# Attended values of two sets made back to back, and a turned-probability buffer of eight units instead of four

## The chip, the core and the metric

The kernel runs on one core of one Trainium2 chip. The metric is the device time in microseconds (us) of one execution. Five engines work side by side: TensorE (PE; its weight loads have a row of their own, PEld), VectorE (DVE), ScalarE (ACT), GpSimd (POOL) and SyncE (SP), which issues the transfers.

## The reference

Seven attention stages run one after the other on x, of shape (8 batches, 112 tokens, 256), with a context of shape (8, 375, 192). Stages 0, 2 and 5 attend to x itself, stages 1, 3, 4 and 6 attend to the context; a feed-forward part follows stages 1, 3 and 6.

```python
h = layer_norm(x)
q = (h @ Wq).reshape(B, 112, 16, D); k = (ctx @ Wk).reshape(B, 375, 16, D); v = (ctx @ Wv).reshape(B, 375, 16, D)
attn = softmax(einsum('bnhd,bshd->bhns', q, k) * scale)
out  = einsum('bhns,bshd->bnhd', attn, v)          # the attended values
x = out.reshape(B, 112, 16 * D) @ Wo + bo + x
```

Stages 1, 3 and 4 are the large cross stages: 16 heads of D = 64 with 375 keys. The change is about them.

## The kernel before

All work is cut into events, and every engine runs a list of them in a fixed order. The order of TensorE is written out by `tensor_order` (L414). The orders of the other engines come from `plan` (L563), which plays the events through with assumed durations. On each engine it takes the event that can start first, and among those that can start at once the one with the smallest value of ready time minus a head start (`AHEAD`, L496). The head start is 2.5 for the copies of turned probabilities (`trans`) and for the value and query evictions, and 0 for the exponentials (`scores`). So on a busy ScalarE these copies go ahead of exponentials.

A unit of a large cross stage is one head of one batch. A set is four units, so a batch has four sets. In this text slot s.b.i is the stretch of TensorE's list from set i of batch b in stage s up to the next set; i = 0 and 2 are the even slots, i = 1 and 3 the odd ones. A unit goes through this chain:

1. `set`: TensorE makes the scores of four units into the four PSUM banks pS, two pairs of units one after the other. From batch 2 on, each unit takes three matmuls (64 rows, 376 columns). A pair may start when ScalarE has read the four-units-older scores out of its banks (`bank_read`, L1192).
2. VectorE takes the maximum (L1826), ScalarE the exponential and its sum (L1696, into P), VectorE the reciprocal (L1850), GpSimd the scaling of P (L1969).
3. `trans`, in the slot after the set: TensorE turns P into a bank of pG in three transposes (L1512), and ScalarE copies it to the turned probabilities PT (L1709). The copy waits until the set that used the same part of PT has been attended (L1704).
4. `av`: TensorE multiplies the turned probabilities of a set with the values V into the bank pO (64 columns of the array for each head, two heads side by side, 24 matmul records in a set). Two sets fill the bank; then ScalarE and VectorE take it out (`ao`, L1715 and L1862).

Between these stands other work (`fill`): keys of the next batch (`k`, `kk`), queries, values (`v`, `vp`), the output projection of an older batch (`wo`). It shares the three banks of pG in turn with the transposes: an event may start when the event three places before it has been evicted (`work_start`, L1324). One piece of the values of each half (`m` = 1) is made in pO, between the two uses of that bank by `av`, at the end of the odd slots (`vp`).

The list `held` in `tensor_order` decides where `av` stands. In slot n stands the `av` of the set before the last one, directly behind the scores of slot n: every slot has one. Two neighbouring slots of TensorE's list, as before has them:

```
set3.4.0 av3.3.2 trans3.3.12 trans3.3.13 v3.4.0m2 trans3.3.14 k3.5.0 trans3.3.15 k3.5.1 kk3.5.0
set3.4.1 av3.3.3 trans3.4.0 trans3.4.1 trans3.4.2 trans3.4.3 k3.5.2 k3.5.3 vp3.4.1m1 v3.4.1 v3.4.1m1 kk3.5.2m1
```

(Stage, batch and then the set, unit or tile.) Batches with an odd number have two query pieces more in every slot except those of batch 7, and slots i = 2 from batch 2 on have `wo`.

Of the kernel before, what the change touches and what calls it, by code (L numbers as in the profile page):

```python
# [9 lines left out]
B, T, C = 8, 112, 256  # L10
# [19 lines left out]
def make_stages():  # L30
    W = 1024
    L0s = dict(i=0, self_=True, small=False, ln=0, res=0, q=(0, 0, W), k=(1, 0, W), v=(2, 0, W), o=(3, 0, C),
               qscale=0.125, escale=1.0, nscale=1.0)
    L0c = dict(i=1, self_=False, small=False, ln=1, res=1, q=(4, 0, W), k=(0, 0, W), v=(1, 0, W), o=(2, 0, C),
               qscale=0.125, escale=1.0, nscale=1.0)
    L1s = dict(i=2, self_=True, small=False, ln=3, res=3, q=(1, 0, W), k=(2, 0, W), v=(3, 0, W), o=(4, 0, C),
               qscale=0.125, escale=1.0, nscale=1.0)
    L1c = dict(i=3, self_=False, small=False, ln=4, res=4, q=(0, 0, W), k=(1, 0, W), v=(2, 0, W), o=(3, 0, C),
               qscale=0.125, escale=1.0, nscale=1.0)
    L2c = dict(i=4, self_=False, small=False, ln=6, res=6, q=(2, 0, W), k=(3, 0, W), v=(4, 0, W), o=(0, 0, C),  # L40
               qscale=1.0, escale=1.0, nscale=0.125)
    L3s = dict(i=5, self_=True, small=True, ln=7, res=7, q=(1, 0, W), k=(1, 512, W), v=(2, 0, 512), o=(2, 1024, C),
               qscale=0.25, escale=1.0, nscale=1.0)
    L3c = dict(i=6, self_=False, small=True, ln=8, res=8, q=(3, 0, 512), k=(4, 0, 512), v=(4, 1024, 512), o=(3, 1024, C),
               qscale=1.0, escale=-0.25, nscale=1.0)
    return [Stage(**s) for s in (L0s, L0c, L1s, L1c, L2c, L3s, L3c)]
# [87 lines left out]
STAGES = make_stages()  # L134
# [12 lines left out]
def set_of(U):  # L147

    s, b, u = UNITS[U]
    return Ev("av", s, b, u // SHAPES[s].GS)  # L150
# [14 lines left out]
def turned_place(U):  # L165

    s = UNITS[U][0]
    if s == 6:
        return "QF", U % 4 * CHUNK, 3 * T
    if s == 5:  # L170
        return "hi", (4 + U % 4) * HC, CHUNK
    if STAGES[s].self_:
        return "PT", U % 2 * CHUNK, CHUNK
    return "PT", U % 4 * 3 * T, 3 * T


def there_before(U, place):
# [32 lines left out]
def joined(s, b):  # L210

    return s in (1, 3, 4) and 0 < b < B


def values_joined(s, b, o):


    return s in (1, 3, 4) and 0 < b < B - o
# [185 lines left out]
def between(work, turned, first, more=0):  # L404

    out = []
    at = [first + n * (len(work) - first + more) // len(turned) for n in range(len(turned))]
    for i in range(len(work) + 1):
        out += [e for e, a in zip(turned, at) if a == i]
        out += work[i:i + 1]  # L410
    return out


def tensor_order():  # L414


    sets = [Ev("set", s, b, i) for s in range(7) for b in range(B) for i in range(SHAPES[s].NS)]
    order = [Ev("lnt", 0, 0), Ev("lnt", 0, 1)] + [Ev("qk", 0, 0, t) for t in range(5)]
    scored, held = [], []
    for n, d in enumerate(sets):  # L420

        if d.s == 5 and d.b < 3:
            order += [held.pop(0), d]
        else:
            order.append(d)
            if len(held) > 1:
                order.append(held.pop(0))
        if n == 0:
            order += [Ev("qk", 0, 0, t) for t in range(5, 8)] + [Ev("v", 0, 0, 0), Ev("v", 0, 0, 1)]
        work = fill(d.s, d.b, d.i)  # L430

        ffs = [n for n, e in enumerate(work) if e.kind in ("ffg", "ffa")]
        if ffs and (d.i == 3 or (d.s, d.i) == (6, 2)):
            order += work[ffs[0]:]
            work = work[:ffs[0]]
            ffs = []
        early = work[:ffs[1]] if len(ffs) > 1 else work
        if joined(d.s, d.b + 1):
            keys = [Ev("k", d.s, d.b + 1, 2 * d.i + j) for j in range(2)]

            qs, rest = [e for e in early if e.kind == "q"], [e for e in early if e.kind != "q"]
            early = [e for pair in zip_longest(qs, rest) for e in pair if e]
            o = (d.s, d.b + d.i // 2, 1 - d.i // 2)
            joint = keys[0]._replace(kind="kk")
            if d.i % 2 and values_joined(*o):

                order += (between(early, scored, 0) if scored else early) + keys
                order += [Ev("vp", *o, 1), Ev("v", *o, 0), Ev("v", *o, 1), joint._replace(m=1)]
            else:
                order += (between(early, scored[:-1], 0, 1) if scored else early) + keys[:1] + scored[-1:] + keys[1:] + [joint]  # L450
        else:
            order += (between(early, scored, 0) if scored else early) + work[len(early):]
        scored = [Ev("trans", d.s, d.b, u) for u in SHAPES[d.s].units(d.i)]
        held.append(Ev("av", d.s, d.b, d.i))
        if d.s in FFS and d.b == B - 1 and d.i == SHAPES[d.s].NS - 1:
            order += tail(d.s, held, scored)
            scored, held = [], []
    return order


def tail(s, held, scored):

    ff = FFS[s]
    if s == 6:
        out = [held[0]] + scored + [Ev("lnt", ff.ln, NTILE - 2), held[1], Ev("ta", s, B - 1), Ev("tb", s, B - 1), Ev("ff2", s, 0), Ev("wo", s, NTILE - 1), Ev("ff2", s, 1), Ev("lnt", ff.ln, NTILE - 1), Ev("ff2", s, 2)] + [Ev("ffg", s, 1, t) for t in range(8)] + [Ev("ff2", s, 3), Ev("ff2", s, 4), Ev("ff2", s, 5), Ev("ff2", s, 6)]
        return out
    nxt = STAGES[s + 1]
    value = [Ev("ffa", s, 0, t) for t in range(3, 8)]
    out = [held[0]] + scored[:3] + value[:1] + scored[3:] + value[1:3] + [held[1]] + value[3:] + [Ev("wo", s, NTILE - 1)]
    out += [Ev("ff2", s, b) for b in range(3)]  # L470
    out += [Ev("lnt", ff.ln, NTILE - 1), Ev("ff2", s, 3), Ev("lnt", nxt.ln, 0)]
    if nxt.self_:
        opening = [[Ev("qk", nxt.i, 0, t)] for t in range(8)]
        values = []
    else:
        opening = [[Ev(kind, nxt.i, 0, t) for kind in ("q", "k")] for t in range(8)]
        values = [Ev("v", nxt.i, 0, 0, m) for m in range(3)]
    for t in range(8):
        out += [Ev("ffg", s, 1, t), Ev("ffa", s, 1, t)]
        if t == 0:  # L480
            out.append(Ev("lnt", nxt.ln, 1))
        elif t > 1:
            out += opening.pop(0)
        if t in (3, 5):
            out.append(Ev("lnt", nxt.ln, 2 + t // 4))
    return out + opening.pop(0) + opening.pop(0) + (values if s == 3 else [])
# [76 lines left out]
def plan():  # L563

    pe = tensor_order()
    pieces = [e for e in pe if e.kind in PIECES]
    item_pieces = {}
# [297 lines left out]
def program(nc, x_in, ctxT, wts, lnp, bo, bff, bsm, lo_rows, mask_s, mask_x, out):  # L865
    F32, F32R, I32, U8 = mybir.dt.float32, mybir.dt.float32r, mybir.dt.int32, mybir.dt.uint8
    ACT, ALU, AX = mybir.ActivationFunctionType, mybir.AluOpType, mybir.AxisListType
    order, stats, norms = plan()
# [48 lines left out]
    with ExitStack() as ctx:  # L917
        def sb(name, shape, dt=F32):
            return ctx.enter_context(nc.sbuf_tensor(name, shape, dt))
# [28 lines left out]
        whole_f = nc.alloc_sbuf_tensor_at("whole_f", [128, 16 * HC], F32, offset=place)  # L948
        AOT_hi, AOT_lo = sb("AOT_hi", [128, 8, 2 * TOK], F32R), sb("AOT_lo", [128, 8, 2 * TOK], F32R)
        P = sb("P", [128, 6 * SP])  # L950
        PT = sb("PT", [128, 4 * 3 * T])

        ao_raw, ao_rows = PT[:, CHUNK:2 * CHUNK], PT[0:T, 0:C]
        src = sb("src", [128, 2, 3 * SP], F32R)
# [227 lines left out]
        def turned(U):  # L1182

            buf, a, n = turned_place(U)
            V = there_before(U, turned_place)
            if buf == "QF":
                view = QF[:, 2 * (U % 4):2 * (U % 4) + 2, :].rearrange("p t n -> p (t n)")
            else:
                view = (PT if buf == "PT" else hid_hi_f)[:, a:a + n]
            return view, 0 if V is None else av_no[set_of(V)]  # L1190
# [959 lines left out]
```

## Time and profile before

| | us |
|---|---|
| median of 3 runs | 1566.91 (1565.21 to 1569.74) |
| the profiled execution, its own time | 1568.49 |
| its span | 1566.5 |
| PE busy in the span | 1504.4 (96%) |
| PEld busy | 1309.2 (84%) |
| ACT busy | 1026.4 (66%) |
| DVE busy | 923.4 (59%) |
| POOL busy | 811.6 (52%) |

The times of the trace count from the start of the span. TensorE is busy almost throughout, so what matters is how long each piece holds it and where it waits for others.

### The profile page before, as it was taken

The numbers are of one execution on the slowest core, as the hardware profiler recorded it, in microseconds if no ns is written. First come the engines' busy times: TensorE is split into PE (matmuls) and PEld (weight loads), VectorE is DVE, ScalarE is ACT, GpSimd is POOL, SyncE is SP. The second block draws the span as 40 slices with busy tenths as digits, with TensorE's granted clock in tenths as the row PEclk, the third lists the DMA queues.
The fourth block names the chain that finished last, engine by engine and source line by source line (L and its number), as shares of the span: only waits on it lengthen the run. The fifth ranks groups of instructions, "written<-read, shape, count | busy, mean of one in ns | idle before, by whom it ended". The sixth has DMA issues, their size and how long they took to land.

```text
span 1566.5 us, 37250 instructions
## 1 busy us (share of the span) xinstructions
PE 1504.4 (96%) x13750; PEld 1309.2 (84%) x13750; DVE 923.4 (59%) x2494; ACT 1026.4 (66%) x2986; POOL 811.6 (52%) x1340
## 2 busy tenths in 40 slices
PE   7999999999999999999999999999999988799998
PEld 6888788888889889888888889878888877677778
DVE  7666544545567655654545557644545568867774
ACT  6666677667652655666667772556667678688871
POOL 3665357666553544446676744346676742433321
PEclk9999999999999999999999999999999999999999
DMA  5233210001120200211001110111000111011000
GB/s 172 86 97 108 69 32 19 19 19 45 43 62 28 72 2 15 68 49 36 18 19 32 45 57 31 55 45 36 18 19 29 37 58 41 24 34 34 19 2 24
DMA packets 41619, 67.26 MB, mean 43 GB/s; under 512 B 8352, under 2 KB 16352, under 8 KB 41440
## 3 DMA queue, kind: packets, MB, share of 16 engines
q1 hardware_dynamic: 40848, 64.71, 13.0%
q8 instruction: 111, 1.82, 0.5%
q14 instruction: 68, 0.56, 0.1%
q10 hardware_dynamic: 592, 0.17, 0.1%
HBM read 59.33 MB, written 5.54 MB: 41 GB/s over the span
## 4 chain that ended last, share of the span: by engine, by line
PE 84%; DVE 7%; ACT 4%; issue 3%; POOL 1%; DMA 1%; SPq 0%; ACTq 0%; DVEq 0%
PE pG L1316 49%; PE pO L1316 12%; PE pG L1512 12%; PE pS L1316 10%; DVE KF L1844 1%; ACT P L1696 1%; DVE nmax L1841 1%; PE pG L1569 1%; DVE W L1774 1%; DVE full L1908 1%; DVE nmax L1826 1%; DVE P L1839 0%; DVE bn L1756 0%; ACT QF_hi L1640 0%; POOL hT_hi L2036 0%
## 5 line engine op out<-in xcount | busy, mean ns | idle before, releaser
L1969 POOL TENSOR_SCALAR P<-P,rinv 112x375 f32<-112x375 f32 (+1 forms) x640 | 323.0, 518 | 261.6 <-DVE rinv L1850 261.3
L1696 ACT ACTIVATE P<-pS,nmax 112x375 f32<-112x375 f32 (+1 forms) x640 | 308.5, 498 | 99.5 <-DVE nmax L1826 99.4
L1316 PE MATMUL pG<-hT_hi,W 128*128 128x224 f32 (+2 forms) x1312 | 299.4, 307 | 8.7 <-DVE hT_lo L1915 4.5
L1709 ACT ACTIVATE PT<-pG 125x336 f32<-125x336 f32 (+1 forms) x448 | 198.7, 470 | 80.9 <-PE pG L1512 80.0
L1316 PEld LDWEIGHTS pG<-hT_hi,W 128*128 128x128 f32 x1312 | 223.5, 193 | 22.2 <-DVE W L1774 4.7
L1512 PE MATMUL pG<-ident,P 112*125 112x112 f32 (+1 forms) x1472 | 226.6, 279 | 13.7 <-ACT PT L1709 5.3
L1826 DVE TENSOR_REDUCE nmax<-pS 112x1 f32<-112x375 f32 (+1 forms) x448 | 227.8, 549 | 7.4 <-PE pS L1316 5.9
L1512 PEld LDWEIGHTS pG<-ident,P 112*125 112x125 f32 (+1 forms) x1472 | 186.6, 176 | 46.6 <-ACT PT L1709 7.5
L1316 PE MATMUL pG<-src,W 128*128 128x376 f32 (+1 forms) x956 | 222.0, 355 | 1.2 <-DVE full L1908 0.5
L1316 PE MATMUL pG<-hT_lo,W 128*128 128x224 f32 (+2 forms) x656 | 195.5, 298 | 0.0
L1316 PEld LDWEIGHTS pG<-src,W 128*128 128x128 f32 (+1 forms) x956 | 160.0, 190 | 28.8 <-issue 25.2
L1316 PE MATMUL pG<-W,src 128*125 128x512 f32 (+2 forms) x645 | 168.5, 383 | 3.1 <-DVE AOT_lo L1881 2.2
L1316 PEld LDWEIGHTS pO<-PT,V 125*64 125x64 f32 (+1 forms) x2816 | 135.8, 137 | 35.6 <-issue 19.4
L1316 PE MATMUL pO<-PT,V 125*64 125x112 f32 (+1 forms) x2816 | 163.3, 264 | 0.8 <-ACT V L1682 0.7
L1850 DVE RECIPROCAL rinv<-rsum 112x1 f32<-112x1 f32 (+1 forms) x448 | 71.7, 161 | 138.3 <-ACT P L1696 134.5
L1996 POOL TENSOR_TENSOR rest<-whole_f,KF_hi 128x376 fp32r<-128x376 f32 x144 | 143.3, 995 | 12.0
L1696 ACT ACTIVATION_READ_ACCUMULATOR P<-pS,nmax 112x1 f32 x640 | 139.6, 218 | 0.0
L1316 PEld LDWEIGHTS pG<-hT_lo,W 128*128 128x128 f32 x656 | 126.3, 193 | 3.2
L1316 PEld LDWEIGHTS pG<-W,src 128*125 128x125 f32 (+1 forms) x645 | 109.1, 186 | 21.4 <-DVE AOT_lo L1881 2.9
L2031 POOL TENSOR_TENSOR rstd<-ve,mhalf 128x1 f32<-128x1 f32 x70 | 44.1, 630 | 153.2 <-DVE ve L1761 153.0
L1994 POOL TENSOR_SCALAR KF_hi<-whole_f 128x376 fp32r<-128x376 f32 x144 | 74.1, 514 | 89.5 <-DVE whole_f L1793 78.8
L1316 PE MATMUL pG<-W,AOT_hi 128*128 128x256 f32 x616 | 115.8, 288 | 1.8 <-DVE AOT_lo L1862 1.1
(139 smaller groups left out, 2893.6 us busy)
## 6 DMA issues: line engine op xcount, KB each, us to landing
wraw<-wts SPq DMA_DIRECT2D x110, 256.0 KB, 2.6
src<-ctx_split SPq DMA_DIRECT2D x64, 282.0 KB, 3.1
ctx_split<-hid_lo_t SPq DMA_DIRECT2D x8, 564.0 KB, 3.5
whole_f<-wts SPq DMA_DIRECT2D x14, 256.0 KB, 6.0
V<-ctxT SPq DMA_DIRECT2D x8, 376.0 KB, 3.8
src_half<-ctx_split SPq DMA_DIRECT2D x21, 94.0 KB, 3.2
bo_b<-bo SPq DMA_DIRECT2D x10, 128.0 KB, 3.2
wraw<-wts SPq DMA_DIRECT2D x8, 64.0 KB
```

Of the source, the lines that this page charges most:

```text
L1316: return nc.tensor.matmul(o, l, r, start=first, stop=last)
L1512: ins = nc.tensor.transpose(g[0:sh.krows, i * T:(i + 1) * T], lhsT, ident[0:T, 0:T])
L1569: ins = nc.tensor.transpose(g[:, k * TOK:(k + 1) * TOK], hn[:, n % 2, k * 128:(k + 1) * 128], ident[:, :])
L1696: ins = act.activation(o, pS[U % 4][0:T, i * n:(i + 1) * n], ACT.Exp, bias=nmax[:, r, i:i + 1], accum_out=rsum[:, r, i:i + 1])
L1709: act.activation(o[0:sh.krows, 0:n], g[0:sh.krows, 0:n], ACT.Copy).then_inc(pt_ready, 1)
L1774: dve.tensor_tensor(o, view, chunk(n, 0)[0].bitcast(F32), ALU.subtract).then_inc(w_lo, 1)
L1826: dve.tensor_reduce(nmax[:, r, 0:sh.G], ps, AX.X, ALU.max, negate=True).then_inc(maxed, 1)
L1850: dve.reciprocal(rinv[:, r, 0:sh.G], rsum[:, r, 0:sh.G]).then_inc(recip, 1)
L1969: ins = pool.tensor_scalar(o, o, rinv[:, r, i:i + 1], st.nscale, ALU.mult, ALU.mult)
L1994: pool.tensor_scalar(KF_hi[:, t, :], keys_rest(t, whole_f), 1.0, 1.0, ALU.mult, ALU.mult).then_inc(k_part, 1)
L1996: pool.tensor_tensor(keys_rest(t), keys_rest(t, whole_f), KF_hi[:, t, :].bitcast(F32), ALU.subtract).then_inc(k_split, 1)
L2031: pool.tensor_tensor(rstd[:, r:r + 1], ve[:, r:r + 1], mhalf[:, :], ALU.pow).then_inc(ln_rstd, 1)
```

## The change

In the large cross stages the list holds back attended values until three sets are held, and then emits two of them together. The even slots have no `av` any more, the odd slots have two, directly behind the scores. So the `av` of sets 0 and 1 of a batch both stand in its slot 3, and those of sets 2 and 3 both in slot 1 of the next batch. PT holds eight units instead of four.

```diff
@@ turned_place
-    return "PT", U % 4 * 3 * T, 3 * T
+    return "PT", U % 8 * 3 * T, 3 * T
@@ tensor_order
         else:
             order.append(d)
-            if len(held) > 1:
+            if held and not STAGES[held[0].s].self_ and held[0].s < 5:
+                if len(held) > 2:
+                    order += [held.pop(0), held.pop(0)]
+            elif len(held) > 1:
                 order.append(held.pop(0))
@@ program
-        PT = sb("PT", [128, 4 * 3 * T])
+        PT = sb("PT", [128, 8 * 3 * T])
```

The same events are run as before. The lists of ScalarE, VectorE and GpSimd come out of `plan` anew from the changed list of TensorE.

## Rows read from the trace of the kernel before

**Rows 1.** The page: span and busy time of each engine, clock by slices.
```profile
span 1566.5 us, 37250 instructions
PE 1504.4 (96%) x13750; PEld 1309.2 (84%) x13750; DVE 923.4 (59%) x2494; ACT 1026.4 (66%) x2986; POOL 811.6 (52%) x1340
PEclk9999999999999999999999999999999999999999
```

**Rows 2.** Slots 3.4.0 to 3.4.2: us, busy PE, PEld, DVE, ACT, POOL (instructions), clock, DMA.
```profile
788.77:795.53 6.76, 6.76 (x66) 5.87 (x63) 3.02 (x9) 5.75 (x16) 5.12 (x8) 1.00 0.00 0
795.53:803.35 7.82, 7.82 (x71) 6.67 (x69) 3.57 (x11) 4.89 (x15) 5.44 (x9) 1.00 0.01 2
803.35:812.99 9.64, 9.64 (x89) 8.76 (x87) 4.45 (x14) 5.97 (x16) 5.84 (x9) 1.00 0.23 72
```

**Rows 3.** Timeline, PE only, slot 3.4.2, three narrow windows: start, us, instructions merged.
```profile
804.20 0.35 PE L1316 MATMUL pS<-KF_hi,rest 64*112 64x376 f32 x2
804.48 0.41 PE L1316 MATMUL pO<-PT,V 125*64 125x112 f32 x4
...
804.63 0.74 PE L1316 MATMUL pO<-PT,V 125*64 125x112 f32 x12
...
805.40 0.46 PE L1316 MATMUL pO<-PT,V 125*64 125x112 f32 x6
805.78 0.58 PE L1512 MATMUL pG<-ident,P 112*125 112x112 f32 x3
```

**Rows 4.** Timeline, PE, slots 4.0.1 (no av) and 4.0.2 (with av).
```profile
1000.56 0.80 PE L1316 MATMUL pS<-KF,QF 64*112 64x376 f32 x4
1001.29 0.58 PE L1512 MATMUL pG<-ident,P 112*125 112x112 f32 x3
...
1011.64 0.80 PE L1316 MATMUL pS<-KF,QF 64*112 64x376 f32 x4
1012.37 0.79 PE L1316 MATMUL pO<-PT,V 125*64 125x112 f32 x11
```

**Rows 5.** Timeline of slots 3.4.0 and 3.4.1, cut; brackets: idle before, and releaser.
```profile
788.98 0.60 ACT L1682 ACTIVATE V<-pO 125x512 f32<-125x512 f32 x1 [2.68 <-PE pO L1316]
...
789.89 1.16 PEld L1316 LDWEIGHTS pO<-PT,V 125*64 125x64 f32 x24 [0.26 <-ACT V L1682]
...
794.14 0.58 ACT L1696 ACTIVATE P<-pS,nmax 112x375 f32<-112x375 f32 x1
...
794.69 0.46 ACT L1709 ACTIVATE PT<-pG 125x336 f32<-125x336 f32 x1
...
795.53 0.33 PE L1316 MATMUL pS<-KF_hi,QF_hi 64*112 64x376 f32 x2
...
796.04 0.34 PE L1316 MATMUL pS<-KF_hi,QF_hi 64*112 64x376 f32 x2
...
796.64 0.68 PEld L1316 LDWEIGHTS pO<-PT,V 125*64 125x64 f32 x14 [0.25 <-issue]
```

**Rows 6.** Busy time by stretch: slots 3.3.0, 1.1.0, 4.7.0, 3.6.0, 3.6.1; columns of Rows 2.
```profile
750.79:758.88 8.09, 8.09 (x79) 7.21 (x76) 3.86 (x11) 6.96 (x20) 5.28 (x8) 1.00 0.01 2
...
198.04:206.37 8.33, 8.33 (x75) 6.92 (x72) 3.80 (x11) 6.95 (x20) 2.56 (x5) 1.00 0.09 31
1244.21:1251.12 6.91, 6.74 (x67) 5.77 (x64) 3.70 (x9) 6.15 (x18) 5.00 (x8) 1.00 0.18 60
859.15:865.89 6.74, 6.74 (x65) 5.86 (x63) 3.55 (x9) 6.12 (x17) 4.68 (x7) 1.00 0.23 79
865.89:874.14 8.25, 7.93 (x71) 6.66 (x71) 4.28 (x13) 5.43 (x18) 6.20 (x9) 1.00 0.19 67
```

**Rows 7.** Waits of the whole trace: who waited for whom, total, times, longest.
```profile
PEld pO L1316 <- ACT V L1682: 12.6, 39, 0.6
...
PE pG L1512 <- POOL P L1969: 5.0, 3, 1.9
```

**Rows 8.** Timeline, PEld, slot 1.7.0.
```profile
408.62 0.48 PEld L1316 LDWEIGHTS pO<-PT,V 125*64 125x64 f32 x9 [0.63 <-ACT V L1682]
```

## The prediction

> **What bounds the kernel now.** I read the page first. TensorE is busy in 96% of the span, no other engine in more than 66%, and the clock is at its upper level, 2.4 GHz, in nearly all slices [rows 1]. So time can only come from what TensorE itself does, or from stalls of TensorE that go or come. The second view is busy time by slot. In slots 3.4.0 to 3.4.2 TensorE is busy for all of 6.76, 7.82 and 9.64 us [rows 2], so there is no stall to take away in a regular slot. But ScalarE is busy for 5.75 of the 6.76 us of slot 3.4.0, and only for 4.89 of 7.82 in the next. The short even slots (i = 0) are the places where a second engine is close to being the bound. The third view is the timeline around one av, which gives its price to a hundredth.
>
> **What an av costs alone, and in a pair.** In slot 3.4.2 the last scores start at 804.20, the first values at 804.48 and the first transposes behind them at 805.78 [rows 3]. The av holds TensorE for 805.78 - 804.48 = 1.30 us. Inside it a pair of matmuls follows the last at an even step: the second pair starts at 804.63, the tenth at 805.40, 0.77 us for 8 steps, 0.096 us each. Twelve pairs at that step are 1.15 us. So 0.15 us of each av is its edge: the first pair takes 0.15 instead of 0.096 (804.48 to 804.63), and behind the last pair, which starts near 805.59, the transposes start 0.19 later instead of 0.096.
>
> What stands in front of the av is not saved. From the scores to the values it is 0.28 us, where a step inside the scores is 0.17 us (three steps from 795.53 to 796.04 [rows 5]). But the transposes would pay it in its place. In slot 4.0.1, which has no av today, the transposes start 0.73 us behind the start of the last four scores (1000.56 to 1001.29), and in 4.0.2 the av starts 0.73 behind them (1011.64 to 1012.37) [rows 4]. So an even slot loses 1.30 us, and the odd slot gains 1.15. The saving of a pair is 0.15 us.
>
> The Trainium skill says, in "TensorEngine Tiling (Array Packing)", Key Properties, that a change of the tiling mode drains the array. The rows agree in that every border costs about 0.1 us. By this rule a pair saves one border of three, and the sum is the one above.
>
> **How many pairs.** held is empty or holds a self-attention set at the start of a stage, so the first pair comes in slot 3 of batch 0. From then on there is one in every odd slot: 8 of (set 0, set 1) and 7 of (set 2, set 3) in a stage. The last two sets of a stage leave as before (the tail of stages 1 and 3, the first slots of stage 5). 15 pairs in 3 stages are 45, and 45 x 0.15 = 6.8 us. No instruction is added and no transfer moves to another queue; the weights (SP) and the context wait for the same events as before, at most one slot's 1.3 us earlier or later.
>
> **The wait that seems to be saved.** The list of waits has 12.6 us of weight loads for pO that waited for ScalarE's copy of V, 39 times [rows 7]. All of these are even slots, and the change takes the av out of them. I cost this at nothing. In slot 3.4.0 the loads stood idle for 0.26 us "for ACT V", and in 3.4.1, where no V is due, 0.25 us for "issue" [rows 5]. It is the border, which stays. Only in slots of batch 7 is it real: 0.63 us instead of 0.26 in 1.7.0 [rows 8], so up to 0.4 us in each of three places. I take 0.5 us in all, since what ScalarE is late with there it will be late with anyway; the bounds are 0 and 1.2.
>
> **The wait that comes.** An even slot loses 1.30 us of TensorE but nothing of ScalarE. Its transposes come 1.3 us sooner behind the scores, and the next set with them. The second pair of the next set, 0.51 us behind its first (795.53, 796.04 [rows 5]), waits for the slot's last exponential. Today that one ends at 794.72, 1.3 us before it is wanted. It is last but one in ScalarE's list, and the list will defer it more: the copies of PT have a head start of 2.5 in the plan and now come ready before the exponentials. Queued behind a stalled second pair are all of TensorE's next events, so each stall is lost for good.
>
> ScalarE starts on a slot 0.21 us in (788.98), has 5.75 us to do, and ends 0.46 sooner if its last item is a copy of PT. The need is at slot length + 0.51. With g for the gaps in which it waits for TensorE (0.41 today: 788.98 + 5.75 would be 794.73, and it ends at 795.15):
> - Slots 2.0 and 4.0 (batch, set): 0.21 + 5.75 + g against 5.46 + 0.51. That is g - 0.01, so 0 to 0.4; I take 0.35, for the exponentials at the end.
> - Slots 3.0 and 5.0, with queries: 7.17 + g against 6.79 + 0.51 [rows 6], g - 0.13; I take 0.2.
> - Slots 1.0 and 1.2: 7.16 + g against 7.03 + 0.51, a margin of 0.38; nothing.
> - Slot 6.0, with a chunk of weights on ScalarE: 6.33 + g against 5.44 + 0.51, 0.38 + g. I take 0.7, less 0.3 for what slot 6.1 loses today (busy 7.93 of 8.25 us, [rows 6]), so 0.4.
> - Slots i = 2 of batches 2 to 6 hold the output projection, 9.64 us with 5.97 of ScalarE [rows 2]: nothing. Those of batches 0 and 7, and 7.0 in stages 1 and 3, hold other long work of TensorE.
> - Slot 4.7.0: 6.36 + g against 5.61 + 0.51, 0.24 + g; I take 0.6.
>
> A stage has 2 x 0.35 + 2 x 0.2 + 0.4 = 1.5 us; three stages and 4.7.0 make 5.1, less the 0.5 above: 4.6 us. Bounds: 0 (a copy of PT last, no gaps) and 21 tight slots (seven in a stage) x 0.8 = 17 us (what ScalarE would be late by if two more copies or evictions stood before the last exponential).
>
> **What else moves, and costs nothing.** The transposes of a set still stand one slot and two avs behind it, so GpSimd has as long as before; it is busy for 5.12 + 5.44 of 14.58 us [rows 2]. The odd slots have 1.15 us more for the same work of ScalarE. With eight units, a copy to PT waits for a set attended in the slot before or at the start of its own. With four it would have waited for an av that now comes later; that is the cover of the second line of the change. The bank pO is emptied at the same point of the odd slot, and vp is still behind four transposes and two key pieces. In the tails, transposes of the last set waited up to 1.9 us for GpSimd [rows 7]; the set in front of them comes 1.3 us sooner, the work between grows by 1.15. I take nothing, with 1 us either way. ScalarE's lists are made anew, and weight chunks may land elsewhere: 1 us either way.
>
> **Sum.** -6.8 + 4.6 = -2.2 us. The profiled execution took 1568.49 us with a span of 1566.5, 1.6 us above the median of 1566.91. The difference is laid on the median: 1564.7 us.
>
> **The rivals.**
> A. The forecast: the edges are saved and the short slots give back 2 to 11 us. 1562 to 1571 us. For it: ScalarE's 5.75 us against a slot of 5.46.
> B. The short slots stall hardly at all, because the copies land such that the last exponential is in time. -6.8 and up to -1.2 more: 1559 to 1562 us. For it: the margin is 1.3 us today in 3.4.0. Against it: the slots shrink by just this.
> C. ScalarE becomes the bound of the even slots. The place is the second pair of the set behind each of the 21 tight slots. The gain is used up at 6.8 / 21 = 0.32 us a slot, and the kernel is slower by over 0.3% from (6.8 + 4.7) / 21 = 0.55 us. At 0.8 it is 1566.9 - 6.8 + 17 = 1577 us. For it: the plan defers exponentials behind copies, and each is 0.58 us long [rows 5]. Against it: ScalarE's whole work in the slot would be done 0.2 to 0.4 us late at most. The skill's page "TensorEngine Tiling (Array Packing)", PSUM Bottleneck, speaks for this rival: packing speeds up TensorE and not the eviction of its banks, which may become the bound.
> D. The edges aren't saved: two avs meet without a common step, since the second waits for its turned probabilities or for the bank. Then the gain is 0, the stalls stay, 1567 to 1572 us. Against it: its copies of PT are made a slot before.
>
> **Chances.** A 0.46, B 0.28, C 0.18, D 0.08. The measurement can tell about 0.3%, 4.7 us, from no change. B is faster whole, and a part of A (0.07); C is slower whole, and a part of D and A (0.07). So faster 0.35, same 0.40, slower 0.25. The range reaches from B to the lower half of C: 1559 to 1574 us.
>
> **What the profile after will show.** If right: 45 rows of 48 values matmuls in one block of about 2.45 us; scores followed by transposes after 0.26 us in even slots; slot 3.4.0 at 5.4 to 5.9 us and 3.4.1 at 8.9 to 9.0. The list of waits has PE or PEld pS waiting for ACT P, about 5 us over some 15 slots, and the 12.6 us for ACT V have gone. Wrong if the even slots are at 5.46 without waits (B), at 6.3 or more (C), or if an idle stands inside the double block (D). The slots of pair 6.0 and 6.1 are the most exposed to a change in the place of a weight chunk.

## The result and the profile after

The changed kernel takes 1597.73 us (1596.85 to 1601.33, 4 runs) where the kernel before takes 1566.76 (1565.21 to 1569.74, 4 runs): the ratio is 1.0208, with an interval of 1.0188 to 1.0227. It is 31 us slower, and the forecast was 2 us faster.

The page of the changed kernel, its first lines:

```profile
span 1594.9 us, 37252 instructions
PE 1499.6 (94%) x13750; PEld 1303.2 (82%) x13750; DVE 925.2 (58%) x2494; ACT 1023.9 (64%) x2986; POOL 808.6 (51%) x1340
```

TensorE's busy time fell by 4.8 us against [rows 1]. Its span grew by 28.4. So about 33 us of new idle time came. (The lower busy time isn't the pairs' alone: 2.7 us of the fall lie in slot 5.5.0, where nothing is paired; see "What was left over".) The busy times slot by slot say where the idle time is. Slots 3.4.0 to 3.4.3 of the changed kernel, columns as in [rows 2]:

```profile
804.89:810.93 6.04, 5.51 (x43) 4.71 (x41) 2.91 (x8) 5.19 (x14) 4.57 (x7) 1.00 0.00 0
810.93:820.85 9.92, 9.21 (x96) 7.75 (x94) 3.67 (x12) 5.43 (x17) 5.95 (x10) 1.00 0.01 2
820.85:829.76 8.91, 8.38 (x67) 7.57 (x65) 4.53 (x14) 5.97 (x16) 5.82 (x9) 1.00 0.24 76
829.76:839.09 9.33, 9.33 (x98) 8.02 (x96) 4.37 (x13) 4.88 (x14) 7.10 (x11) 1.00 0.01 4
```

The second number of a row is TensorE's busy time. The last slot has no gap and is what the forecast says (8.15 before, plus 1.15, is 9.30). Both even slots have a gap of 0.53 us, and the slot behind the short one a gap of 0.71. The list of waits of the changed kernel names the two:

```profile
PEld pG L1515 <- ACT whole_f L1674: 32.4, 36, 1.4
PE pG L1515 <- ACT whole_f L1674: 19.9, 36, 1.1
PE pS L1319 <- ACT P L1699: 16.8, 20, 1.2
```

(Lines stand three lower than before: L1515 is the transposes, L1674 ScalarE's eviction of a key tile, L1685 its eviction of V, L1699 the exponential.) The list of before has no row in which transposes wait for a key tile, and for matmuls that wait for the exponential only this:

```profile
PE pS L1316 <- ACT P L1696: 2.4, 3, 1.2
```

**The first wait: a cover has gone.** Before, in slot 3.4.0 (timeline, cut; the two evictions of V ahead of the key tile are at 788.98, in [rows 5], and 789.47):

```profile
789.47 0.59 ACT L1682 ACTIVATE V<-pG 125x512 f32<-125x512 f32 x1
...
789.89 1.37 PE L1316 MATMUL pO<-PT,V 125*64 125x112 f32 x24
789.95 0.49 ACT L1671 ACTIVATE whole_f<-pG 128x376 f32<-128x376 f32 x1
...
791.20 0.58 PE L1512 MATMUL pG<-ident,P 112*125 112x112 f32 x3
```

The key tile leaves its bank at 790.44, and the transposes three ring places behind it take that bank at 791.20. The `av` between the scores and the transposes gave 0.76 us of margin. The same place after the change:

```profile
805.05 0.60 ACT L1685 ACTIVATE V<-pO 125x512 f32<-125x512 f32 x1 [2.68 <-PE pO L1319]
...
805.55 0.59 ACT L1685 ACTIVATE V<-pG 125x512 f32<-125x512 f32 x1
...
806.02 0.49 ACT L1674 ACTIVATE whole_f<-pG 128x376 f32<-128x376 f32 x1
...
806.57 0.73 PEld L1515 LDWEIGHTS pG<-ident,P 112*125 112x125 f32 x6 [0.85 <-ACT whole_f L1674]
806.57 0.91 PE L1515 MATMUL pG<-ident,P 112*125 112x112 f32 x6 [0.53 <-ACT whole_f L1674]
```

ScalarE does the same three evictions at the same pace. The transposes now want the bank 1.3 us sooner and it comes free 0.54 us too late for them. The list has 36 such waits, all in even slots: 0.53 or 0.54 us in the thirty of batches 2 to 6, 0.3 in three of batch 1, and 0.9 to 1.1 in three of batch 7.

**The second wait: the last exponential stands behind a key tile.** Slots 3.4.0/3.4.1 of the changed kernel, the border between them (slot 3.4.1 starts at 810.93):

```profile
811.09 0.48 ACT L1674 ACTIVATE whole_f<-pG 128x376 f32<-128x376 f32 x1 [0.57 <-PE pG L1319]
...
811.47 0.57 ACT L1699 ACTIVATE P<-pS,nmax 112x375 f32<-112x375 f32 x1
...
812.24 0.20 PEld L1319 LDWEIGHTS pS<-KF_hi,QF_hi 64*112 64x112 f32 x2 [1.01 <-issue]
...
812.27 0.43 PE L1319 MATMUL pS<-KF_hi,QF_hi 64*112 64x376 f32 x2 [0.71 <-ACT P L1699]
...
812.97 1.75 PE L1319 MATMUL pO<-PT,V 125*64 125x112 f32 x32
```

ScalarE is idle for 0.57 us with an exponential to do. Its list, made anew from TensorE's, reads "... `trans3.3.15 k3.5.0 scores3.4.3`", where before it read "`scores3.4.3 trans3.3.15 k3.5.0`". The key tile `k3.5.0` is complete only with the joint key matmuls at the slot's end, so the exponential of 3.4.3 behind it can't start before the next set does, and that set's second pair waits for it. In batches 2 to 5 of stage 1 the list keeps the exponential in front, and slots 1.2.1 and 1.4.1 take 8.96 and 8.95 us, not 9.92. Why the plan comes out so in stages 3 and 4 and not in stage 1 was not looked into.

**One gain that wasn't forecast.** In slot 4.0.3 before, transposes stood 3 us behind a copy of PT, which was queued on ScalarE behind a weight conversion that waited for its transfer:

```profile
1026.01 0.42 ACT L1625 ACTIVATE W<-wraw 128x256 fp32r<-128x256 f32 x1 [4.45 <-DMA wraw<-wts]
...
1027.81 0.97 PE L1512 MATMUL pG<-ident,P 112*125 112x112 f32 x3 [3.04 <-ACT PT L1709]
```

The wait was paid twice. The granted clock fell while TensorE stood idle there, and the 5.68 us of work behind the wait ran at 0.50 of full speed, the lower level of 1.2 GHz: eight key matmuls took 2.85 us, and 1.64 in the changed kernel. The stretch of before, and under it the whole slot 4.0.3 of c3, a kernel shown further down that pairs nothing:

```profile
1027.81:1033.49 5.68, 5.68 (x18) 5.28 (x19) 2.01 (x8) 3.05 (x10) 3.49 (x6) 0.50 0.19 67
...
1026.82:1035.21 8.39, 8.39 (x69) 6.53 (x68) 5.13 (x14) 5.50 (x16) 3.47 (x6) 1.00 0.46 148
```

So without a wait the slot takes 8.39 us with one `av`, and the 14.00 of before are that, 3.04 of wait and 2.57 of slow clock. In the changed kernel it takes 10.74: 1.15 for the second `av`, 1.07 of wait, and the clock stays at 1.00. The second `av` covers a part of the wait, but the transfer also landed 0.8 us sooner in the slot. In c2 and c3, with one `av` there, ScalarE doesn't wait for the transfer at all, and the slot takes 8.39 us in both. So how much of this gain is the pair's isn't shown, and why the transfer lands where it does is open.

### The profile page after: what moved, and what is told of

It reads as the page before. It is cut to its first block, busy times and chain, and to the rows that moved or that the text cites. A ratio compares the mean times of both kernels' runs of the same rounds, so it can differ in the third digit from the quotient of the medians.

```text
span 1594.9 us, 37252 instructions
## 1 busy us (share of the span) xinstructions
PE 1499.6 (94%) x13750; PEld 1303.2 (82%) x13750; DVE 925.2 (58%) x2494; ACT 1023.9 (64%) x2986; POOL 808.6 (51%) x1340
## 4 chain that ended last, share of the span: by engine, by line
PE 79%; ACT 7%; DVE 7%; issue 4%; POOL 1%; DMA 1%; ACTq 0%; DVEq 0%
PE pG L1319 48%; PE pO L1319 12%; PE pG L1515 12%; PE pS L1319 7%; ACT P L1699 2%; ACT V L1685 2%; DVE KF L1847 1%; ACT whole_f L1674 1%; DVE nmax L1844 1%; DVE bn L1759 1%; PE pG L1572 1%; DVE x L1891 1%; DVE nmax L1829 0%; DVE P L1842 0%; ACT QF_hi L1643 0%
## 5 line engine op out<-in xcount | busy, mean ns | idle before, releaser
L1699 ACT ACTIVATE P<-pS,nmax 112x375 f32<-112x375 f32 (+1 forms) x640 | 308.0, 496 | 96.0 <-DVE nmax L1829 96.0
L1515 PE MATMUL pG<-ident,P 112*125 112x112 f32 (+1 forms) x1472 | 224.5, 278 | 32.0 <-ACT whole_f L1674 19.9
L1515 PEld LDWEIGHTS pG<-ident,P 112*125 112x125 f32 (+1 forms) x1472 | 185.7, 176 | 73.8 <-ACT whole_f L1674 32.4
L1319 PE MATMUL pO<-PT,V 125*64 125x112 f32 (+1 forms) x2816 | 153.7, 262 | 0.2
L1699 ACT ACTIVATION_READ_ACCUMULATOR P<-pS,nmax 112x1 f32 x640 | 139.0, 217 | 0.0
```

The lines of the kernel that those rows point to most:

```text
L1319: return nc.tensor.matmul(o, l, r, start=first, stop=last)
L1515: ins = nc.tensor.transpose(g[0:sh.krows, i * T:(i + 1) * T], lhsT, ident[0:T, 0:T])
L1699: ins = act.activation(o, pS[U % 4][0:T, i * n:(i + 1) * n], ACT.Exp, bias=nmax[:, r, i:i + 1], accum_out=rsum[:, r, i:i + 1])
```

## The experiments

The experiments on ScalarE's list are edits of the list behind `order, stats, norms = plan()`, so TensorE's order stays as it is.

**e1: only the key tiles first.** The changed kernel, with ScalarE's key tile of the odd slots ahead of the two evictions of V.

```diff
+    act_list = order["act"]
+    for e in [e for e in act_list if e.kind == "k" and by_act(e) and e.i % 4 == 2]:
+        n = act_list.index(e)
+        m = n
+        while act_list[m - 1].kind == "v":
+            m -= 1
+        act_list.insert(m, act_list.pop(n))
```

> The changed kernel with one thing moved in ScalarE's list: at the border from an odd to an even slot it evicts the key tile first and the two pieces of values after it (the list had values, values, keys). Theory 1 (the transposes of the even slot, which now follow the scores directly, wait for the bank of that key tile, 0.55 us 36 times, 19.9 us in the list of waits): these waits go, about 20 us less than the changed kernel, 1576 to 1580 us. Rival (ScalarE as a whole is too slow for the shortened slots, whatever its order): the time stays within 5 us of 1598 us, since the last exponential of the slot then takes the wait over.

1579.58 us, ratio to before 1.0087 (1.0072 to 1.0103). The changed kernel's ratio is 1.0208, so this is 19 us less. The windows of slots 3.4.0 and 3.4.1:

```profile
797.77:803.27 5.50, 5.50 (x41) 4.68 (x39) 2.91 (x8) 4.98 (x14) 4.49 (x7) 1.00 0.00 0
803.27:813.19 9.92, 9.21 (x94) 7.76 (x94) 3.67 (x12) 5.44 (x17) 6.06 (x10) 1.00 0.01 2
```

The first gap is gone and the second is untouched. Over the large cross stages 39 even slots are shorter than in the changed kernel, by 0.36 to 0.63 us each and 19 us together (the 36, and the first even slot of batch 1 in each stage).

**e2: only the exponentials first.** The changed kernel, with the last exponential of a slot ahead of the next batch's key tile.

```diff
+    for e in [e for e in act_list if e.kind == "k" and by_act(e)]:
+        n, u = act_list.index(e), Ev("scores", e.s, e.b - 1, 2 * e.i + 3)
+        if act_list.index(u) > n:
+            act_list.insert(act_list.index(u), act_list.pop(n))
```

> The changed kernel with the other thing moved in ScalarE's list: an eviction of a key tile that stands ahead of the last exponentials of the slot before goes behind them. Theory 2 (in most slots behind set 0 of a batch in stages 3 and 4, and in all of batch 1, the last exponential stands behind a key eviction, which can't start before the last key matmul of that slot; so the second pair of the next set waits 0.7 us or more, 16.8 us over 20 waits in the list): about 13 to 17 us less, 1581 to 1585 us; the 0.55 us waits of the transposes stay. Rival (ScalarE's whole work is the limit): no more than 5 us less.

1581.75 us, ratio 1.0100 (1.0085 to 1.0115), 17 us less than the changed kernel's. The same two slots:

```profile
797.47:803.51 6.04, 5.51 (x42) 4.71 (x39) 2.91 (x8) 5.56 (x16) 4.53 (x7) 1.00 0.00 0
803.51:812.47 8.96, 8.96 (x94) 7.80 (x94) 3.58 (x12) 5.08 (x17) 6.01 (x10) 1.00 0.01 2
```

Here the second gap is gone and the first stays. The slot loses 0.96 us, where the list showed TensorE 0.71 and its loads 1.01 us idle.

**e3 and d1: both.** The two edits together, run twice under two labels.

> Both moves together. If theories 1 and 2 are all of it, what is left of the change is the saved edges, 45 x 0.15 = 6.8 us, and small waits in the short slots of up to 0.4 us: 1560 to 1566 us, faster than the kernel before or the same. Rival (ScalarE's whole work in an even slot, 5.75 us in 5.46 us, is the limit): 1575 us or more.

> The kernel of e3_both once more, since its interval touched no change. Theory (0.15 us saved at each of some 45 pairs, both waits gone, 1 to 2 us given back at the short slots): 1560 to 1566 us, ratio to before 0.996 to 0.999. Rival (the pair saves nothing that the chip gives in the whole): ratio within 0.001 of 1, 1566 to 1568 us.

e3: 1564.11 us, ratio 0.9986 (0.9969 to 1.0004). d1: 1564.23 us, ratio 0.9981 (0.9971 to 0.9992). The two edits take off 35 us together, what e1 and e2 take off one by one (19 + 17). Slots 3.4.0 to 3.4.3 of e3, and its wait for exponentials:

```profile
789.87:795.37 5.50, 5.50 (x41) 4.68 (x39) 2.91 (x8) 5.29 (x16) 4.49 (x7) 1.00 0.00 0
795.37:804.33 8.96, 8.96 (x94) 7.81 (x94) 3.58 (x12) 5.09 (x17) 6.07 (x10) 1.00 0.01 2
804.33:812.66 8.33, 8.33 (x65) 7.59 (x63) 4.50 (x14) 5.75 (x16) 5.82 (x9) 1.00 0.26 81
812.66:821.97 9.31, 9.31 (x97) 8.02 (x97) 4.40 (x13) 4.89 (x14) 7.12 (x11) 1.00 0.01 4
```
```profile
PE pS L1331 <- ACT P L1711: 3.3, 6, 0.8
```

The four slots sum to 32.10 us where before they sum to 32.37: 0.27 for two pairs. TensorE never waits in them. The double block itself, in slot 3.3.1 of e3, TensorE's timeline:

```profile
759.92 2.52 PE L1331 MATMUL pO<-PT,V 125*64 125x112 f32 x48
762.38 0.80 PE L1527 MATMUL pG<-ident,P 112*125 112x112 f32 x5
```

It holds TensorE for 762.38 - 759.92 = 2.46 us, against twice 1.30.

**e4: the second line of the change alone.** The kernel before, with PT of eight units.

```diff
-    return "PT", U % 4 * 3 * T, 3 * T
+    return "PT", U % 8 * 3 * T, 3 * T
...
-        PT = sb("PT", [128, 4 * 3 * T])
+        PT = sb("PT", [128, 8 * 3 * T])
```

> The kernel before with the second line of the change alone: eight units of turned probabilities, the order of TensorE as it was. Theory: it costs and brings nothing, within 2 us of the kernel before, since no copy to the buffer waits for an older set there. Rival (the other places of the buffers in memory or other planned lists of the engines cause part of the loss): slower by 5 us or more.

1566.53 us, ratio 1.0005 (0.9992 to 1.0019). It costs and brings nothing.

**c1: both list edits in the kernel before.** Is the repair of ScalarE's list a gain by itself?

> The kernel before, with its own order of TensorE, and both moves in ScalarE's list (keys before the values, last exponentials before the next slot's keys). Theory (in the kernel before the attended values of the even slot cover the eviction of the keys, so its place in the list doesn't matter): within 2 us of the kernel before; what the paired kernel with both moves gains then belongs to the pairing. Rival (the moves gain by themselves): 4 us or more faster.

1570.16 us, ratio 1.0032 (1.0020 to 1.0043): slower, where the same time was expected. Its list of waits, and its slot 3.4.0:

```profile
PEld pO L1328 <- ACT V L1694: 18.9, 39, 1.0
```
```profile
792.20:799.15 6.95, 6.82 (x66) 5.89 (x63) 3.02 (x9) 5.75 (x16) 5.09 (x8) 1.00 0.00 0
```

In the order of before, the `av` stands directly behind the scores and needs the bank pO free of V. With the key tile evicted first, V comes 0.5 us later and the slot grows from 6.76 to 6.95, as thirty even slots do by about 0.2 us; three of batch 7 grow by 0.36 to 0.39. The wait of [rows 7] was 12.6 us there and is 18.9 here. So in the kernel before V rightly went first, with little to spare, and in the paired one the key tile has to. No one order of ScalarE's evictions suits both places of the `av`.

**c2 and c3: the cover alone, without a pair.** The order of before, with eight units in PT, and the single `av` of an even slot placed behind the slot's first two transposes. c3 adds e1's edit.

```diff
+            late = None
             if len(held) > 1:
-                order.append(held.pop(0))
+                late = held.pop(0)
+                if not (late.s == d.s and d.i % 2 == 0 and joined(d.s, d.b + 1)):
+                    order.append(late)
+                    late = None
+        at = len(order)
...
+        if late:
+            turns = [m for m in range(at, len(order)) if order[m].kind == "trans"]
+            order.insert(turns[1] + 1, late)
```

> No pairing: every slot keeps its attended values, the buffer has eight units, and in 39 even slots the attended values stand behind the slot's first two transposes instead of in front of them. Theory (they were the cover of the key eviction; what is lost is the cover, not something of the pairing): the first transposes wait for ScalarE's key copy again, some 0.55 us in each of 39 slots, 21 us, and one more border between array shapes, 0.1 to 0.2 us each, 4 to 8 us: 1588 to 1598 us. Rival (the loss comes from the double block in the odd slots or from the shorter even slots): 1571 to 1575 us.

> The same as the run before, with ScalarE evicting the key tile before the two pieces of values. Theory: the 0.55 us waits go and the extra border stays: 1570 to 1577 us. Rival (the transposes wait for something else): as slow as the run before.

c2: 1590.23 us, ratio 1.0157 (1.0142 to 1.0173). c3: 1571.45 us, ratio 1.0039 (1.0024 to 1.0053). The list of waits of c2, then slot 3.4.0 of c2 and of c3:

```profile
PE pG L1521 <- ACT whole_f L1680: 16.8, 33, 0.5
```
```profile
804.63:812.15 7.52, 6.99 (x66) 5.94 (x63) 3.07 (x9) 5.87 (x16) 5.24 (x8) 1.00 0.00 0
```
```profile
793.49:800.41 6.92, 6.92 (x67) 5.94 (x64) 3.07 (x9) 5.76 (x16) 5.25 (x8) 1.00 0.00 0
```

Nothing is paired here, and each even slot keeps its `av`. The wait for the key tile comes all the same, as soon as the `av` isn't in front of the first transposes, and goes when the tile is evicted first. What c3 keeps is 0.16 us a slot (6.92 against 6.76) without a wait: between two transposes the `av` has one border more. The second slots of batch 0 (3.0.2 and its like), in which TensorE waits in neither kernel, grow by as much, from some 9.87 to some 10.05 us. The Trainium skill says in "TensorEngine Tiling (Array Packing)", Key Properties, that a change of the tiling mode drains TensorE; the slots agree, with some 0.17 us for one border more.

**c4: exponentials with a head start.** e3, and in `ahead` the exponentials of the sets i = 0 and 2 get the 2.5 that the copies have.

```diff
+    if engine == "act" and e.kind == "scores" and joined(e.s, e.b + 1) and e.i // 4 % 2 == 0:
+        return 2.5
```

> The paired kernel with both moves, and the plan gives the exponentials of even slots the head start of 2.5 that the copies of turned probabilities have, so that they are spread between these. Theory (what the paired kernel with both moves still loses is the order in the slots with queries: 0.34 us in each of 6 pairs of slots in batch 1 and 0.17 us in 6 more even slots): 1 to 3 us less than it, 1561 to 1563 us. Rival (those waits are ScalarE's whole work): no difference.

1572.18 us, ratio 1.0041 (1.0028 to 1.0053): 8 to 9 us slower than e3, where 1 to 3 us less were expected. Slot 3.4.0 takes 6.06 us, not 5.50, as the copies of PT and the evictions from the ring now stand behind exponentials. Only the places where e3 still waits for exponentials gain: slot 3.6.1 goes from 9.95 to 8.98, the double slots of batch 1 from 11.03 to 10.69 (before plus 1.15). In a tight slot each order of ScalarE's list is late for somebody, and the ring's bank is wanted first.

**d2: V of the ring before V of pO.** d1, with the three evictions in the order key tile, ring's V, pO's V.

```diff
-        act_list.insert(m, act_list.pop(n))
+        act_list[m:n + 1] = act_list[m:n + 1][::-1]
```

> As d1_both_again, but in a slot with an odd-slot eviction ahead of it ScalarE's three evictions stand in the order key tile, projection's V, attended values' V, so the last, which nothing waits for soon in the paired order, goes last. Theory: the first transposes of the even slots of batches that also have query pieces take the bank of the projection's V; these 12 or so slots came out about 0.17 us short of the full saving in e3_both, and would get it back; 2 to 3 us less than d1_both_again, near 1561 us, ratio to before near 0.996. Rival (these slots are held by something other than that eviction): the same time as d1_both_again within 0.5 us.

1563.75 us, ratio 0.9980 (0.9970 to 0.9991): the same as d1, and slot 3.3.0 stays at 6.96 us. The theory fell, the bank's V wasn't late. d1's timeline of slot 3.3.0 shows another neighbour:

```profile
753.29 0.58 PE L1527 MATMUL pG<-ident,P 112*125 112x112 f32 x3
...
753.72 0.59 ACT L1711 ACTIVATE P<-pS,nmax 112x375 f32<-112x375 f32 x1
...
754.26 0.47 ACT L1724 ACTIVATE PT<-pG 125x336 f32<-125x336 f32 x1
...
754.39 0.48 PE L1527 MATMUL pG<-ident,P 112*125 112x112 f32 x3
...
754.79 1.43 PE L1331 MATMUL pG<-W,src 128*125 128x512 f32 x5
```

The projection of V at 754.79 uses the bank of the transposes at 753.29. Their copy ends at 754.73, as an exponential went ahead of it.

**d3: that copy before that exponential.**

```diff
+    for e in [e for e in act_list if e.kind == "scores" and e.s in (1, 3, 4) and e.b in (3, 5) and e.i % 8 == 0]:
+        n = act_list.index(e)
+        if act_list[n + 1].kind == "trans":
+            act_list.insert(n, act_list.pop(n + 1))
```

> The kernel of d1_both_again, and in the even slots of batches 3 and 5 of the three large stages (12 slots) ScalarE copies the first turned probabilities before the slot's first exponential, not behind it. In d1_both_again the projection of V there starts 0.40 us behind the start of the transposes ahead of it, where the kernel before had 0.25, just after that copy ends (754.73, 754.79): it uses the bank that the copy empties. Theory: the 0.17 us by which these slots fall short of a saving of 1.30 us (8.09 to 6.96) is this copy; they come to about 6.80 us, 12 x 0.16 = 2 us in all, near 1562 us, ratio to before 0.996 to 0.998. Rival (the slot is held by something else, or the exponential deferred by 0.47 us takes the same time elsewhere): the slots stay at 6.96 or their successors grow, 1564 us.

1561.74 us, ratio 0.9967 (0.9953 to 0.9981): faster than the kernel before. The same place in d3:

```profile
752.03 0.58 PE L1531 MATMUL pG<-ident,P 112*125 112x112 f32 x3
...
752.65 0.45 ACT L1728 ACTIVATE PT<-pG 125x336 f32<-125x336 f32 x1
...
753.13 0.48 PE L1531 MATMUL pG<-ident,P 112*125 112x112 f32 x3
753.38 1.40 PE L1335 MATMUL pG<-W,src 128*125 128x512 f32 x5
```

The projection starts 0.25 us behind the transposes ahead of it, not 0.40, as before the change. The six slots i = 0 came from 6.96 to 6.85 us, the six i = 2 from 9.82 to 9.73, 1.2 us in all, and their successors stayed. The direction and the place are as expected, and the size is a little over half: 0.04 to 0.07 us a slot are not explained. The step from d1's ratio to d3's is 0.0014, 2 us, and the two intervals overlap. That d3 beats the kernel before is shown by its own interval, that it beats d1 only by the slots. How much of the former is the pairs' is another question; see "What was left over".

## Why the prediction was wrong

**"The saving of a pair is 0.15 us": right.** The block is 2.46 us, an unhindered even slot lost 1.25 to 1.31 us and an odd one gained 1.15, and two pairs save 0.27 us in slots 3.4.0 to 3.4.3. 45 pairs at 0.15 are the 6.8 us. TensorE's busy time in e3, 1498.8 us, is 5.6 under [rows 1], but that doesn't measure the saving: 2.7 us of it lie in slot 5.5.0 and 1.3 in 4.0.3, where the clock differs. The count of borders beside the sum is off: an `av` in each of two slots has four, a pair and the bare border of the even slot have three, so one of four goes, not one of three. The sum doesn't use it. Rival D is out: the second `av` follows without a gap.

**"The wait that seems to be saved" costed at nothing: right about the price, incomplete about the place.** The 12.6 us for ACT V gave no time back: the even slots without a stall shrank by no more than the `av`. But c1 shows that V's eviction was nearly late there: half a microsecond later, and 0.2 us of it is paid in each of thirty even slots.

**"What else moves, and costs nothing": this step failed, by 19 us.** The prediction asked of the transposes only when P is ready (GpSimd's side) and found as much time as before. It didn't ask for the bank that they write. The rule for that stands in the description of the kernel before: an event may start when the event three ring places before it has been evicted. For the first transposes of an even slot that is a key tile, third in ScalarE's list at the slot's start. The `av` that was taken away was the cover: 1.30 us taken from a margin of 0.76 leaves the bank 0.54 us late, in slots such as 3.4.0, and e1 gives back 19 us over 39 even slots. The 1.30 and the 0.76 stand in the trace of before, but the row of the key tile's eviction (789.95) was none of those that the sum rests on. e1 removes this wait and nothing else, c2 makes it without any pair, c3 removes it there.

**"The wait that comes": right kind of wait, right place in part, term mis-sized.** The prediction had the second pair wait for the last exponential, and took 0.2 to 0.6 us a slot from ScalarE's total of work, 4.6 us in all. Measured were 0.96 us in slots such as 3.4.1, and 17 us in all. Of the 18 waits that are new, six stand in batch 1, where it took nothing, and in stage 1 the slots of batches 2 to 5 have none. ScalarE's total isn't the cause: in e3 it is busy for 5.29 us of a slot of 5.50 and TensorE doesn't wait, so the term of 0.35 us for slots 2.0 and 4.0 is 0. What costs is the order: an instruction that waits for the end of TensorE's slot stands in front of one that was ready. The prediction said "the list will defer it more", and then counted only copies ahead of the exponential, which take ScalarE's time, not a key tile, which waits for TensorE. e2 takes this out: 17 us.

**Rival C** had the place, the price point (slower from 0.55 us a slot) and the sign. Its mechanism, ScalarE as the bound of the even slots, is refuted by e3, and its 17 us match the 16.8 of the list by chance. Its 0.18 was too low: nothing in the trace excluded an order of the list worse than the work. The first wait was in no rival. The range ended at 1574 us, 24 under the result, and C's own figure of 1577 is 21 under.

**What was left over.** e3 and d1 come to 2 to 3 us under before, not 6.8. Slot by slot in d1, against a saving of 1.30 in an even slot and a gain of 1.15 in an odd one:

| where | us given back | shown by |
|---|---|---|
| double slots of batch 1, five of six, 0.33 each | 1.7 | c4 takes it out: exponentials |
| slots 1.6.1, 3.6.1, 4.6.1, some 0.6 each | 1.8 | c4 takes it out: exponentials |
| slot 4.7.1 | 0.5 | not tried |
| even slots of batches 3 and 5, twelve, about 0.16 each | 1.9 | d3 takes out 1.2 of it |
| even slots of batch 7, five of six, 0.3 each | 1.4 | not tried |

That is some 7 us, all of the gain: the 89 slots of the pairs other than 4.0.3 sum to 0.8 us less in d1 than before. What d1 has under before lies elsewhere. Its span is 5.2 us shorter. Slot 4.0.3 is 4.0 us shorter (14.00 to 10.04), see above, and slot 5.5.0 in stage 5, where nothing is paired, 2.8 us. The last is clock: in before it was granted 0.70 in the mean there, in the changed kernel 1.00.

```profile
1316.77:1328.29 11.52, 10.79 (x113) 9.66 (x113) 8.03 (x18) 7.36 (x22) 1.71 (x4) 0.70 0.01 2
...
1347.72:1356.42 8.70, 8.07 (x113) 6.80 (x113) 7.72 (x18) 7.38 (x22) 1.71 (x4) 1.00 0.01 3
```

d1 takes 8.70 us there too, and so does c1 (8.69), which pairs nothing. On the other side, the first scores come 1.0 us later in d1, and slot 2.0.0 takes 1.35 us more, as it does in e4, again without a pair (12.19 against 10.65 us). Such steps of 1 to 3 us come and go between the profiles of kernels that don't differ in these places. So the 3.0 us of d1's ratio, with bounds of 1.3 and 4.5, are not shown to be the pairs': their slots come out nearly even, and the rest is one wait for a transfer, which a second `av` fills in part, and the clock. The prediction had no term for 4.0.3: it took the transposes' waits to be GpSimd's, in the tails, and there was a 3 us one for ScalarE.

**Eight units in PT: right.** e4 shows no cost.

## What to carry to other kernels

Work that is moved away from in front of another piece was cover for everything which that piece waits for: its input, and also the buffer it writes, and who empties that and in which order. For each piece that will start sooner, take the time of the last release of each of its resources from the trace and subtract. When the order of the bound engine changes, make the lists of the helper engines part of the change: an instruction in an in-order list that waits for the end of a stretch holds all that stands behind it, however little work the engine has. And before a difference between two kernels is put down to the change, look where in the span it lies: here two slots hold more than all of d1's lead, and the change doesn't touch one of them.

## What was not expected of the hardware

An `av` between two transposes costs 0.16 us more than one between scores and transposes (c3, 6.92 against 6.76 us), with the same matmuls. And a stall of the second pair is longer than TensorE's idle row: 0.71 us in the row, 1.01 in that of the weight loads, 0.96 in the length of the slot; the slot's length is the measure. And a wait can cost nearly twice its row: behind the 3.04 us in slot 4.0.3 of before the clock was granted at 0.50 for 5.68 us of work, which cost 2.57 us more by the difference to the same slot of c3.
